# Layer one's contexts as 64 by 32 products, eight at once, and the dense part's pieces in the order gate, up, down, gate, down, up, down, down

## The reference

```
layer zero: h = rms(x) * (w * (1 + cond @ tw.T))            # 8 query heads of 64, 1 key/value head
            x = x + softmax(rope(q) rope(k).T / 8) v @ Wo.T
            h = rms(x) * (...)
            x = x + (silu(h @ Wg.T) * (h @ Wu.T)) @ Wd.T    # 512 -> 2048 -> 512
layer one:  h = layernorm(x) * (1 + scale) + shift          # 16 query heads of 32, 4 key/value heads
            c = h @ Wkd.T;  k = c @ Wku.T;  v = c @ Wvu.T
            y = softmax(rope(q) rope(k).T / sqrt(32)) v     # a sequence of 64 rows lies inside the window
            x = x + y @ Wo.T
```

## Time and profile before

| | us |
|---|---|
| median of 3 timed runs | 870.33 (867.33 to 871.2) |
| profiled execution | 865.27 |
| its span, first to last instruction | 863.5 |
| PE busy in the span | 843.4 (98%) |
| DVE, ACT, POOL busy | 596.1 (69%), 442.7 (51%), 405.0 (47%) |
| PE's share of the chain that ended last | 76% |

### The profile page before, as it was taken

One profiled execution on the slowest core, in us unless ns is written; L12 is line 12 of the kernel. 1 busy time (PEld: TensorE's weight loads), 2 busy tenths in 40 slices (PEclk: granted clock), 3 DMA queues, 4 the chain that ended last, 5 costly groups with the idle time before them and its releaser, 6 DMA issues.

```text
span 863.5 us, 15478 instructions
## 1 busy us (share of the span) xinstructions
PE 843.4 (98%) x5864; PEld 702.7 (81%) x5864; DVE 596.1 (69%) x877; ACT 442.7 (51%) x819; POOL 405.0 (47%) x320
## 2 busy tenths in 40 slices
PE   9899999999999999999999999999999999999997
PEld 5787888888888888888787888888878878887885
DVE  6787466666666666666457788776856857767876
ACT  4666445455345455444447556446364454445662
POOL 2466545545544545547357545445343434432331
PEclk9999999999999999999999999999999999999999
DMA  9902534533523533533534446446345264240001
GB/s 346 359 25 74 165 114 111 173 119 105 180 97 98 178 121 93 177 105 116 195 117 122 143 159 180 134 131 194 107 146 171 88 181 131 72 130 13 27 27 37
DMA packets 114297, 113.53 MB, mean 131 GB/s; under 512 B 57520, under 2 KB 80048, under 8 KB 114224
## 3 DMA queue, kind: packets, MB, share of 16 engines
q1 hardware_dynamic: 113504, 112.45, 40.9%
q10 hardware_dynamic: 720, 0.09, 0.1%
HBM read 88.15 MB, written 24.38 MB: 130 GB/s over the span
## 4 chain that ended last, share of the span: by engine, by line
PE 76%; DVE 7%; issue 6%; POOL 4%; ACT 4%; DMA 3%; SPq 0%; POOLq 0%; ACTq 0%; DVEq 0%
PE ps L685 23%; PE ps L687 22%; PE ps L686 22%; PE ps L799 2%; PE ps L965 2%; DMA pT<-turned_p 1%; PE ps L731 1%; PE ps L776 1%; DVE ex L1410 1%; PE ps L722 1%; DMA turned_q<-tq 1%; PE ps L942 1%; POOL qkr L592 1%; POOL qkr L591 1%; ACT yf L1841 1%
## 5 line engine op out<-in xcount | busy, mean ns | idle before, releaser
L685 PE MATMUL ps<-h2h,guh 128*128 128x512 f32 x512 | 204.2, 399 | 2.1 <-issue 1.2
L687 PE MATMUL ps<-h2l,guh 128*128 128x512 f32 x512 | 199.8, 390 | 0.0
L686 PE MATMUL ps<-h2h,gul 128*128 128x512 f32 x512 | 199.6, 390 | 0.0
L544 POOL TENSOR_TENSOR gul<-rgu,guh 128x1024 fp32r<-128x1024 f32 x64 | 161.0, 2516 | 71.8 <-ACT guh L1749 71.8
L549 POOL TENSOR_TENSOR wdl<-rwd,wdh 128x512 fp32r<-128x512 f32 x64 | 82.8, 1294 | 141.3 <-ACT wdh L1757 141.3
L1309 DVE TENSOR_TENSOR xres<-ps,xres 128x512 f32<-128x512 f32 x128 | 87.6, 685 | 63.5 <-PE ps L687 62.8
L685 PEld LDWEIGHTS ps<-h2h,guh 128*128 128x128 f32 x512 | 96.1, 188 | 23.5 <-issue 2.9
L687 PEld LDWEIGHTS ps<-h2l,guh 128*128 128x128 f32 x512 | 96.1, 188 | 20.7
L686 PEld LDWEIGHTS ps<-h2h,gul 128*128 128x128 f32 x512 | 96.2, 188 | 19.3
L685 PE MATMUL ps<-wdh,ah 128*128 128x512 f32 x256 | 100.3, 392 | 2.3 <-DVE al L1304 1.1
L686 PE MATMUL ps<-wdh,al 128*128 128x512 f32 x256 | 99.7, 389 | 0.0
(11 more groups left out here) (178 smaller groups left out, 1670.6 us busy)
## 6 DMA issues: line engine op xcount, KB each, us to landing
rgu<-gu SPq DMA_DIRECT2D x64, 512.0 KB, 4.7
rwd<-WdT SPq DMA_DIRECT2D x64, 256.0 KB, 3.9
turned_q<-tq SPq DMA_DIRECT2D x20, 320.0 KB, 3.1
qkT<-turned_q SPq DMA_DIRECT2D x20, 320.0 KB, 3.7
turned_p<-tp SPq DMA_DIRECT2D x9, 512.0 KB, 2.6
pT<-turned_p SPq DMA_DIRECT2D x9, 512.0 KB, 3.8
xt<-xT SPq DMA_DIRECT2D x16, 256.0 KB, 3.2
out<-xres SPq DMA_DIRECT2D x15, 256.0 KB, 3.6
```

The costliest lines, as they stand in the source:

```text
L544: pool.tensor_tensor(gul[i][:, :], rgu[i][:, :], guh[i][:, :], ALU.subtract).then_inc(m_gul, 1)
L685: pe.matmul(dst, lh, rh, start=start, stop=False)
L686: pe.matmul(dst, ll, rh, start=False, stop=False)
L687: return pe.matmul(dst, lh, rl, start=False, stop=stop)
```

## The change

Two independent parts. First, the contexts of layer one. The values are stored without the zeros (`v1`), and a product has K = 64 rows (the 64 keys of one head parity), M = 32 columns (one value head) and 128 moving columns (two query heads of one sequence). There are again 16 products for a tile, but each sits in one of eight places of the array, 64 rows by 32 columns, and the loops walk through all eight before a place is used again. The two row halves write to two banks, so the context also takes the bank that project1 of the step before may have written: context1 waits for b_out. y_T's wait changes from b_pTb to b_ch and b_cl. The two memsets on POOL go; the columns of Wo are put in the new order on the host.

Second, a pair's pieces come in the order gate, up, down, gate, down, up, down, down. DVE, ACT, POOL and SP move their parts accordingly; on ACT the last slot of a pair now makes the high part of the activation ahead of that of the down weights.

```diff
-        bdv1 = [sb(f"bdv1_{i}", [P, 2, KT, 2 * HD1]) for i in range(2)]
+        v1 = [sb(f"v1_{i}", [P, 2, KT, HD1]) for i in range(2)]
+        sb("pad2", [P, 4 * KT * HD1])
...
-            return banks1(NT - 2)[h]
+            return banks1(NT - 2 + h)[0]
...
+        def ctx_view1(k):
+            return ps[:, k, 0:D // 2].rearrange("p (i w f) -> p i w f", i=2, w=W)
+
+        def both(t):
+            at = banks1(t)[2]
+            return ps[:, at:at + 2, 0:D // 2].rearrange("p r (i n) -> p r i n", i=2)
+
+        def by_pair(ap):
+            return ap.rearrange("p (i r) n -> p r i n", r=2)
 
...
-            def clear_bdv1():
-                pool.wait_ge(a_rope, NT)
-                for i in range(2):
-                    pool.memset(bdv1[i][:, :, :, :], 0.0).then_inc(b_zero, 1)
...
             def mlp():
                 for p in range(NP):
-                    for n in (2 * p, 2 * p + 1):
-                        for w in range(2):
-                            gate_or_up(n, w)
-                            yield
-                            if p:
-                                down(p - 1, 2 * (n % 2) + w)
-                                yield
+                    gate_or_up(2 * p, 0)
+                    yield
+                    gate_or_up(2 * p, 1)
+                    yield
+                    if p:
+                        down(p - 1, 0)
+                        yield
+                    gate_or_up(2 * p + 1, 0)
+                    yield
+                    if p:
+                        down(p - 1, 1)
+                        yield
+                    gate_or_up(2 * p + 1, 1)
+                    yield
+                    if p:
+                        down(p - 1, 2)
+                        yield
+                        down(p - 1, 3)
+                        yield
...
-                pe.wait_ge(b_pTb, t - 2 - TAIL)
+                else:
+                    pe.wait_ge(b_ch, t - 2)
+                    pe.wait_ge(b_cl, t - 2)
...
-                for j in range(KT):
-                    for b in range(2):
-                        for i in range(2):
-                            mm = pe.matmul(ps[S * i:S * (i + 1), banks1(t)[2],
-                                              P * j + S * b:P * j + S * (b + 1)],
-                                           bdv1[t % 2][:, b, j, :], pT1[:, 2 * b:2 * b + 2, 2 * j + i, :],
-                                           start=True, stop=True)
+                if t < TAIL:
+                    wait(pe, b_out, t)
+                for b in range(2):
+                    for r in range(2):
+                        for j in range(KT):
+                            rows, heads = slice(S * r, S * (r + 1)), pT1[S * r:S * (r + 1), :, 2 * j:2 * j + 2, :]
+                            to = ctx_view1(banks1(t)[2 + r])[HD1 * j:HD1 * (j + 1), :, 2 * b:2 * b + 2, :]
+                            mm = pe.matmul(to, v1[t % 2][rows, b, j, :],
+                                           heads[:, 2 * b:2 * b + 2].rearrange("p w i f -> p i w f"),
+                                           start=True, stop=True, tile_position=(S * r, HD1 * j))
...
+                pe.wait_ge(b_ds, 2 * NT)
+                for b in range(2):
+                    for r in range(2):
+                        for j in range(KT):
+                            rows = slice(S * r, S * (r + 1))
+                            mm = pe.matmul(ps[HD1 * j:HD1 * (j + 1), last_ctx(h) + r, S * b:S * (b + 1)],
+                                           v1[t % 2][rows, b, j, :], pT1[rows, 2 * b:2 * b + 2, 2 * j + h, :],
+                                           start=True, stop=True, tile_position=(S * r, HD1 * j))
...
+                    yield
+                    low_act(2 * p)
                     if p:
                         add_down(p - 1, 0)
                         yield
-                    multiply(2 * p)
-                    yield
-                    low_act(2 * p)
+                    yield
                     if p:
                         add_down(p - 1, 1)
                         yield
+                    multiply(2 * p + 1)
                     yield
                     if p:
                         add_down(p - 1, 2)
                         yield
-                    multiply(2 * p + 1)
-                    yield
-                    if p:
                         add_down(p - 1, 3)
                     low_act(2 * p + 1)
...
+                    high_act(2 * p + 1)
                     high_wd(2 * p + 1)
-                    high_act(2 * p + 1)
...
-                dve.tensor_tensor(ycl[:, :, :], by_feature(bank(banks1(t)[2])), yc[:, :, :],
+                dve.tensor_tensor(by_pair(ycl[:, :, :]), both(t), by_pair(yc[:, :, :]),
                                   ALU.subtract).then_inc(b_cl, 1)
...
-                act.copy(yc[:, :, :], by_feature(bank(banks1(t)[2]))).then_inc(b_ch, 1)
+                act.copy(by_pair(yc[:, :, :]), both(t)).then_inc(b_ch, 1)
```

More of the change, by code:

```diff
@@ L191, in build @@
          b_v, b_qkT, b_qka, b_qkb, b_sc, b_max, b_ds, b_ex,
-         b_sum, b_rec, b_p, b_pTr, b_pTa, b_pTb, b_ctx, b_ch, b_cl, b_wo, b_out, b_zero, b_st) = [
+         b_sum, b_rec, b_p, b_pTr, b_pTa, b_pTb, b_ctx, b_ch, b_cl, b_wo, b_out, b_st) = [
             sem("b_" + n) for n in (
             "bn mv var rstd nb xn xT yf hh hl qkv rope qks v qkT qka qkb sc "
-            "max ds ex sum rec p pTr pTa pTb ctx ch cl wo out zero st").split()]
+            "max ds ex sum rec p pTr pTa pTb ctx ch cl wo out st").split()]
         def bank(k):
@@ L640, in _ @@
                     rstd1(0)
-                    clear_bdv1()
                 fill(pieces, f1)
@@ L986, in p_T_last @@
                 pe.wait_ge(b_p, NT + h)
-                for j in (2 * h, 2 * h + 1):
-                    for i in range(2):
-                        mm = pe.transpose(ps[:, banks1(NT - 1)[2 + h], 256 * (j % 2) + P * i:
-                                             256 * (j % 2) + P * (i + 1)],
-                                          ex1[:, j, 2 * i:2 * i + 2, :].rearrange("p g s -> p (g s)"), idn[:, :])
+                for j in range(KT):
+                    mm = pe.transpose(ps[:, banks1(NT - 1)[2 + h], P * j:P * (j + 1)],
+                                      ex1[:, j, 2 * h:2 * h + 2, :].rearrange("p g s -> p (g s)"), idn[:, :])
                 mm.then_inc(b_pTr, 1)
@@ L1000, in context_last @@
                     pe.wait_ge(b_pTb, t - TAIL + 1)
-                for j in (2 * h, 2 * h + 1):
-                    for b in range(2):
-                        for i in range(2):
-                            mm = pe.matmul(ps[S * i:S * (i + 1), last_ctx(h),
-                                              P * j + S * b:P * j + S * (b + 1)],
-                                           bdv1[t % 2][:, b, j, :], pT1[:, 2 * b:2 * b + 2, 2 * j + i, :],
-                                           start=True, stop=True)
+                pe.wait_ge(b_ds, 2 * NT)
+                for b in range(2):
+                    for r in range(2):
+                        for j in range(KT):
+                            rows = slice(S * r, S * (r + 1))
+                            mm = pe.matmul(ps[HD1 * j:HD1 * (j + 1), last_ctx(h) + r, S * b:S * (b + 1)],
+                                           v1[t % 2][rows, b, j, :], pT1[rows, 2 * b:2 * b + 2, 2 * j + h, :],
+                                           start=True, stop=True, tile_position=(S * r, HD1 * j))
                 mm.then_inc(b_ctx, 1)
@@ L1479, in low_ctx_last @@
                     dve.wait_ge(b_wo, NT - 1)
-                dve.tensor_tensor(ycl[:, k, :], by_feature(bank(last_ctx(h)))[:, k, :], yc[:, k, :],
+                dve.tensor_tensor(ycl[:, k, :], ps[:, last_ctx(h):last_ctx(h) + 2, 0:P], yc[:, k, :],
                                   ALU.subtract).then_inc(b_cl, 1)
@@ L1850, in values1 @@
                 if t == 0:
-                    act.wait_ge(b_zero, 2)
+                    act.wait_ge(a_rope, NT)
                 act.wait_ge(b_rope, t + 1)
@@ L1856, in values1 @@
                     for i in range(2):
-                        ins = act.copy(bdv1[t % 2][S * i:S * (i + 1), b, :, HD1 * i:HD1 * (i + 1)]
-                                       .rearrange("p (c j) d -> p c j d", c=2),
+                        ins = act.copy(v1[t % 2][S * i:S * (i + 1), b, :, :].rearrange("p (c j) d -> p c j d", c=2),
                                        ps[S * b:S * (b + 1), at:at + 2, QQ1 + KK1:QK1]
@@ L1870, in softmax_exp1 @@
                     act.wait_ge(b_ds, 2 * t + i + 1)
-                    half = ex1[:, 2 * i:2 * i + 2, :, :]
+                    half = ex1[:, :, 2 * i:2 * i + 2, :] if t == NT - 1 else ex1[:, 2 * i:2 * i + 2, :, :]
                     act.activation(half, half, ACT.Exp, scale=float(HD1) ** -0.5).then_inc(b_ex, 1)
@@ L1887, in probs_T_last @@
                     act.wait_ge(b_ctx, NT - 1)
```

(6 more changed lines are left out.)

42 lines of the change are left out of this document (21 added, 21 removed).

## The result

Before: 868.83 us median of 4 runs; after: 877.35 us (876.55 to 878.71, 4 runs). The ratio is 1.010, 95% interval 1.006 to 1.014. The change makes the kernel about 1% slower. The profiled execution of the changed kernel has a span of 874.8 us, 11.3 more than that of before, at a mean clock of 0.994. On a later chip the same two kernels gave 1.0138 (1.0110 to 1.0167), a difference of 12.1 us.

A forecast was written before the change was run, and what follows sets the result against it. PE's own work was taken to set the time, with its waits added nearly whole. 12.0 + 1.9 + 1.0 + 0.7 - 2.9 - 6.9 = +5.8 us on the median of 870.33 makes 876.1; range 864 to 886.

The forecast's parts named there:

- Contexts: Layer one: each context takes 0.61 us instead of 1.08; with late steps and last halves, 6.9 us gained together.
- the late steps: Layer one, tiles 9 to 14: context and scores together get shorter by 0.4 us a tile, 2.4 us in all.
- the two last halves: The last tile's context, done in two halves: a gain of 0.3 us for both.
- The rival by the rule of the Trainium skill on row groups: Layer one's contexts stay near 1.08 us and gain nothing, since neighbouring products share rows: 883.0 us, chance 0.08.
- The stalls: Layer zero, steps 7, 9, 11, 13: the fourth piece waits for DVE's add, 3.0 us each, 12.0 us in all.
- the lower bound: Stall of 2.7 us a step, if DVE's whole chain moves 1.36 us earlier with the context of the step before.
- Step 15: Layer zero's step without rope or qkv: a stall of 3.0 us, less 1.1 already lost to SiLU, 1.9 net.
- the last four pieces: Layer zero's steps 7 to 15, odd: DVE's add comes about level with PE, 0.2 us in each of five, 1.0.
- The clock: Rival: stalls of 3 us bring half clock, 1.5 us lost each, five times 7.5: 883.6 us, chance 0.15.
- What was taken away: Layer one's waits shortened by the longer way from a pair's last up to the first down needing it: 2.9 us gained.
- the start of layer one: Step 0: the wait for scores gets 1.1 us shorter and the context's wait 0.3 us.
- the wait for `al` in step 5: Layer one: this wait of 1.1 us, which comes from ACT, stays; gain 0.

The follow-up runs named there:

- ctx_only: Changed kernel with the MLP pieces of all five engines in the order of before, so the new contexts alone: 861.75 us, ratio to before 0.9955.
- order_only: Kernel before with the new order of the MLP pieces alone: 884.72 us, ratio to before 1.0212.
- ctx_one: Changed kernel with context loops turned so the four products of one column place follow each other: 876.87 us, one run.
- silu_first: Changed kernel with ACT doing one SiLU ahead of tile preparation in layer zero's even steps from 6 and layer one's steps -1 and 0: 879.37 us, 1.0141.
- ctx_four: Changed kernel with context loops turned: all products of the first 64 rows, then all of the other 64: 874.79 us, one run.
- add_early: Changed kernel with one DVE add moved ahead of the rope products in layer zero's odd steps from 7: 865.29 us, ratio to before 0.9997.
- the mixed order: New contexts, piece order of before for pairs 0 to 19, new order from pair 20: 857.18 us, 0.9916; second run 861.13 us, 0.9935.

## Why the prediction was right

**Bound and direction.** PE's own work sets the time, the contexts give, the order costs more than they give: shown by ctx_only and order_only. Predicted 876.1 us, measured 877.35. That nearness is in part luck. The forecast was a difference of +5.8 us. Measured were 8.5 between the medians, 12.1 on the later chip and 11.3 between the spans, so the cost itself was put too low by a third to a half, and errors of both signs stand in the sum.

**Contexts.** 0.60 us as predicted (0.61), the late steps 0.3 instead of 0.4, the two last halves 0.46 instead of 0.3. The reason given (eight places at once, a round by its columns) is not what ctx_one shows; the number came out since both ways of counting give it. The rival by the rule of the Trainium skill on row groups ("TensorE: Matmul & The Clock Gate", Part 3) is refuted here: 0.60 to 0.64 us, whichever rows stand next to each other. Alone in the kernel they gave 5.3 us by the scores of the last tile and 4.3 in the span, not 6.9: PE met the wait for `al` earlier (2.2 us instead of 1.1), and the clock fell at the end. I had counted such waits only where the order changed.

**The stalls.** The mechanism is right in each part: the fourth piece, the add, the rope ahead of it, steps 7 to 15. The size was 2.3 us in three steps and 1.6 in step 11, where I took 3.0 between bounds of 2.7 and 4.1: 8.6 instead of 12.0. In step 13 the add starts 6.99 us behind the start of the first piece, against 8.80 before, so it moved by 1.8 us against PE and not by 1.36. The 0.45 more is PE's own wait for SiLU ahead of the scores: the chain came 1.36 earlier, as the lower bound had it, and PE came 0.45 later. silu_first shows it by taking that wait away: the stalls are then 2.9. Stall and SiLU wait together are 2.8, the lower bound. I should have taken that bound, since every link from POOL's low part to the add keeps its distance (11.87 and 11.88 us). Step 11 has no SiLU wait ahead of it, and its add came 2.4 us earlier against the scores (12.85 us behind them before, 10.48 now); why the chain moved further there is not shown. Step 15: predicted 3.0 less the 1.1 of SiLU's wait; measured 1.87, with SiLU's wait still there. The 1.0 us for the last four pieces of these steps had no wait behind it: none stands there.

**The clock.** A rival with 0.15, and it came true in part: three falls of 3.4 us instead of five of 3. It was priced rightly by half-clock stretches, but I tied it to stalls of 3 us. Falls came with waits of 2.3 us (steps 7 and 13) and 2.1 (step -1), and none with step 9's stall, neither at 2.35 us nor at 2.9 in silu_first. The length of the one wait doesn't tell whether the clock falls. A stall of this size must be given part of that price in the forecast itself.

**What was taken away.** Here the sum was wrong both ways. I had 1.4 us of gain at the start of layer one, and there the order lost: SiLU waits of 2.1 and 1.3 us, a longer transfer wait and a fall of the clock. I looked at which wait of before would end sooner, and what the new second gate waits for I had put at nothing in layer zero and within 0.7 us in layer one. On the other side the wait for `al` in step 5, which I left at its full length, went (1.3), and so did the one for probabilities in step 6 (1.8, predicted 1.5).

**Terms against each other.** Too high were the stalls (3.4), the last four pieces (1.0) and what stayed of the waits in steps 5 and 6 (1.6). Too low were the clock (5.1), the SiLU waits of layer zero (1.35) and of layer one (3.4 where I had 0.7), and the start of layer one, where I had 1.4 of gain and 1.0 was lost. Together that is 5.6 us too low, and the spans differ by 11.3 where I had 5.8. The medians differ by 8.5 only, since the profiled execution of before lies 3.6 us under the median measured beside the changed kernel, that of the changed kernel 0.8 under its own.

## What to carry to other kernels

When pieces that share two buffers are put in a new order, look for two of them that use the same buffer closer together than before, and find what the consumer's engine does between: here 2.4 us of rope on DVE made the cost, and one piece moved ahead of it gave back 9 to 12 us. A change of order can cost in one phase and gain in another; apply it from the phase in which the trace shows the gain. Taking away a wait on PE gains nothing if PE's next wait is for a chain that was under way on other engines before the first wait ended: the next wait grows by as much. Look for where that chain starts, and price the two waits as one.

## What the runs showed of the hardware

- Waits of PE of 2.32 and 2.34 us (steps 7 and 13) were followed by 3.4 us at half clock, one of 2.35 (step 9) was not. Four more traces with these stalls, the changed kernel again, order_only, silu_first and ctx_one, have the falls in the same two steps; ctx_four has the one in step 13 alone. In silu_first waits of 2.89 (step 9) and 2.54 us (step 15) brought none, and the wait of 2.12 us in step -1 brought one in the changed kernel and none in add_early. In the second trace of the mixed order one stands behind waits of 0.9 and 1.2 us (777 to 780 us). With eight small products in the waits of steps 7 and 13 there was none.
- At the kernel's end, where PE waits three times for 0.7 to 1.1 us, the clock fell in some executions and not in others. From the scores of the last tile to the end it took 14.7 to 14.8 us with the new contexts and no fall (the changed kernel, both traces of the mixed order), 16.3 with one of 3.4 us (ctx_only) and 17.3 with one of 6.8 (add_early, the changed kernel again). So it is worth 1.5 to 2.5 us between executions of one kernel.
- fp32 products of 64 rows by 32 columns with 128 moving columns were issued at 13.6 ns a record (two records a product), in every order of places tried.
